# A graph attention layer on one core: the left scores spread over the partitions by two small transposes and a line in DRAM

## The reference

```python
type_sum = adj @ h0                                  # the b side aggregates h0, then multiplies by W_gcnb
attn_a = sigmoid(concat([type_sum, h0]) @ Wa.T + ba)
attn_b = sigmoid(concat([type_sum, h0]) @ Wb.T + bb)
h = h0 @ W_sa
scores = (h @ a_left)[:, None] + (h @ a_right)[None, :]
e = where(adj != 0, exp(-leaky_relu(scores, 0.01)), 0)
x_a = (e / (sum(e, axis=1) + 1e-5)) @ h
x_b = adj @ (h0 @ W_gcnb) + b_gcnb
out = x + sigmoid(attn_a * x_a + attn_b * x_b)
```

## Time and profile before

| | us |
|---|---|
| median of 3 runs | 181.63 |
| lowest and highest | 180.57, 183.06 |
| the profiled execution | 181.05 |
| its span, first to last instruction | 179.3 |
| PE busy in the span | 173.6 |
| DVE, ACT, POOL busy | 146.9, 116.6, 18.3 |

### The profile page before, as it was taken

One profiled execution on the slowest core, in us unless ns is written; L12 is line 12 of the kernel. 1 busy time (PEld: TensorE's weight loads), 2 busy tenths in 40 slices (PEclk: granted clock), 3 DMA queues, 4 the chain that ended last, 5 costly groups with the idle time before them and its releaser, 6 DMA issues.

```text
span 179.3 us, 3430 instructions
## 1 busy us (share of the span) xinstructions
PE 173.6 (97%) x1337; PEld 127.4 (71%) x1337; DVE 146.9 (82%) x309; ACT 116.6 (65%) x171; POOL 18.3 (10%) x42
## 2 busy tenths in 40 slices
PE   7889999999999999999999999999999999999992
PEld 2456676664544448888854478888888888888892
DVE  3698997638899999799999910999999999987542
ACT  3397989753999988658495630584884785773410
POOL 3645346030000200000000000000000000000000
PEclk9999999999999999999999999999999999999999
DMA  6999999999950598000001100000010010011101
GB/s 140 273 249 195 200 179 175 199 239 236 260 212 4 79 214 176 0 4 2 0 4 59 59 0 4 0 0 4 0 59 4 2 59 0 4 60 59 62 29 29
DMA packets 5199, 15.81 MB, mean 88 GB/s; under 512 B 576, under 2 KB 1344, under 8 KB 4416
## 3 DMA queue, kind: packets, MB, share of 16 engines
q0 software_dynamic: 1584, 8.39, 24.4%
q1 hardware_dynamic: 3600, 7.22, 12.0%
HBM read 21.90 MB, written 2.10 MB: 134 GB/s over the span
## 4 chain that ended last, share of the span: by engine, by line
PE 92%; DMA 3%; DVE 2%; SPq 1%; ACT 0%; issue 0%; DVEq 0%
PE ps L762 31%; PE ps L787 16%; PE ps L786 16%; PE ps L785 16%; PE ps L778 6%; PE ps L736 5%; DMA c_sb<-in_consts 3%; PE ps L725 2%; PE ps L747 1%; SPq L225 1%; PE ps L844 1%; DVE stats L475 0%; DVE nat_lo L510 0%; SPq L230 0%; DVE e_lo L505 0%
## 5 line engine op out<-in xcount | busy, mean ns | idle before, releaser
L785 PE MATMUL ps<-mv_lo,e_hi 128*128 128x257 f16 (+2 forms) x272 | 71.0, 267 | 0.0
L787 PE MATMUL ps<-mv_hi,e_lo 128*128 128x257 f16 (+2 forms) x272 | 70.9, 266 | 0.0
L786 PE MATMUL ps<-mv_hi,e_hi 128*128 128x257 f16 (+2 forms) x272 | 70.8, 266 | 0.0
L351 ACT ACTIVATE z<-z,log_e 128x1024 f32<-128x1024 f32 x32 | 36.7, 1146 | 28.6 <-DVE z L547 28.6
L762 PE MATMUL ps<-adj,nat_hi 128*128 128x512 f16 x128 | 48.5, 379 | 0.6 <-DVE nat_lo L510 0.6
L762 PE MATMUL ps<-adj,nat_lo 128*128 128x512 f16 x128 | 48.5, 379 | 0.0
L547 DVE SCALAR_TENSOR_TENSOR z<-sl_row,exs,far 128x512 f32<-128x512 f32 x64 | 45.1, 745 | 0.0
L555 DVE TENSOR_TENSOR e_lo<-z,e_hi 128x1024 f16<-128x1024 f32 x32 | 39.0, 1219 | 1.3 <-ACT e_hi L361 1.3
L361 ACT ACTIVATE e_hi<-z 128x1024 f16<-128x1024 f32 x32 | 33.3, 1041 | 0.0
L786 PEld LDWEIGHTS ps<-mv_hi,e_hi 128*128 128x128 f16 x272 | 26.6, 98 | 3.2
L785 PEld LDWEIGHTS ps<-mv_lo,e_hi 128*128 128x128 f16 x272 | 26.4, 97 | 3.3
(11 more groups left out here) (69 smaller groups left out, 184.1 us busy)
## 6 DMA issues: line engine op xcount, KB each, us to landing
adj<-in_adj_t POOLq DMA_DIRECT2D x6, 1024.0 KB, 10.4
x_sb<-in_x SPq DMA_DIRECT2D x6, 512.0 KB, 13.8
out<-res SPq DMA_DIRECT2D x7, 256.0 KB, 2.0
adj<-in_adj_t POOLq DMA_DIRECT2D x3, 512.0 KB, 8.8
x_sb<-in_x SPq DMA_DIRECT2D x3, 256.0 KB, 5.1
adj<-in_adj_t POOLq DMA_DIRECT2D x2, 256.0 KB, 6.3
wa_sb<-in_w_wide SPq DMA_DIRECT2D x1, 258.0 KB, 4.8
c_sb<-in_consts SPq DMA_DIRECT2D x1, 258.0 KB, 5.0
```

The costliest lines, as they stand in the source:

```text
L351: act.activation(z[:, n % ZRING, :, :], z[:, n % ZRING, :, :], ACT.Exp, bias=log_e[:, 0:1], scale=SLOPE - 1.0).then_inc(exp_done, 1)
L785: pe.matmul(ps[:, bank, cols], e_hi[:, s, i1], mv_lo[:, j, cols], start=(j == 0), stop=False)
L786: pe.matmul(ps[:, bank, cols], e_hi[:, s, i1], mv_hi[:, j, cols], start=False, stop=False)
L787: return pe.matmul(ps[:, bank, cols], e_lo[:, s, i1], mv_hi[:, j, cols], start=False, stop=(j == NT - 1))
```

## The change

The left scores take another way to sl_row. A transpose `sl_lines(h)` turns eight tiles' SL columns at once (in: 128 partitions x 8; out: 8 partitions x 128, in the last quarter of PSUM bank 2 or 0, which no product uses). ScalarE copies the 8 x 128 values to sl_turn, a piece of part_b that is still free. SP stores them as half a line of 2048 values in DRAM, waits for that, and loads the half line back, broadcast to all 128 partitions (512 KB into sl_row).

The first transpose stands ahead of the wide products of tile 10, the second after the first four neighbour tiles of `b_products(1)`. VectorE waits at n = 0 for the first half line and at n = 16 for the second. On ScalarE the first copy stands in `mv_highs(5)`, the second ahead of wg_hi. On SP the second store stands ahead of the `x_back` loads and the second broadcast load behind them.

```diff
+SL_UNIT = 6
+SL_BANKS = (2, 0)
+SL_COLS = slice(BANK - P, BANK)
...
+        sl_turn = [part_b[0:NT // 2, h, 0:P] for h in range(2)]
...
+            def sl_store(h):
+                sp.wait_ge(sl_moved, h + 1)
+                sp.dma_start(sl_line[h * N // 2:(h + 1) * N // 2].rearrange("(t i) -> t i", i=P), sl_turn[h]).then_inc(sl_stored[h], 16)
+
+            def sl_spread(h):
+                sp.wait_ge(sl_stored[h], 16)
+                half = slice(h * N // 2, (h + 1) * N // 2)
+                sp.dma_start(sl_row[:, half], sl_line[half].partition_broadcast(P)).then_inc(sl_ready[h], 16)
+
+            sl_store(0)
+            sl_spread(0)
+            sl_store(1)
             sp.wait_ge(turned, NU)
             sp.wait_ge(nat_ready, NPAIR)
             for g in range(NG):
                 ts = slice(g * GT, (g + 1) * GT)
                 sp.dma_start(x_sb[:, ts, :], x[:, ts, :]).then_inc(x_back[g], 16)
+            sl_spread(1)
...
             def mv_highs(p):
                 act.wait_ge(exs_ready, p + 1)
+                if p == SL_UNIT - 1:
+                    sl_lines(0)
...
-            def sl_rows(c):
-                act.wait_ge(sl_turned, c + 1)
-                act.activation(sl_row[:, c * CW:(c + 1) * CW], ps[:, c % 2, :], ACT.Copy).then_inc(sl_ready, 1)
+            def sl_lines(h):
+                act.wait_ge(sl_turned, h + 1)
+                act.activation(sl_turn[h], ps[0:NT // 2, SL_BANKS[h], SL_COLS], ACT.Copy).then_inc(sl_moved, 1)
...
             act.activation(factor_l[:, :], exs[:, :, SL], ACT.Exp, scale=SLOPE).then_inc(factors_done, 1)
-            sl_rows(0)
-            sl_rows(1)
+            sl_lines(1)
             act.wait_ge(wg_landed, 16)
...
-                if n == 1:
-                    sl_rows(2)
-                    sl_rows(3)
...
                 if j == 0:
-                    dve.wait_ge(sl_ready, c + 1)
+                    dve.wait_ge(sl_ready[c // 2], 16)
...
+                    if t == UNITS[SL_UNIT][0]:
+                        sl_lines(0)
...
-            def sl_rows(c):
-                pe.wait_ge(exs_ready, 2 * c + 2)
...
-                for t in range(GT):
-                    ins = pe.transpose(ps[:, c % 2, t * P:(t + 1) * P],
-                                       exs[:, c * GT + t, SL:SL + 1].broadcast_to([P, P]), ident[:, :])
-                ins.then_inc(sl_turned, 1)
+            def sl_lines(h):
+                pe.wait_ge(exs_ready, 4 * h + 4)
+                pe.transpose(ps[0:NT // 2, SL_BANKS[h], SL_COLS], exs[:, h * NT // 2:(h + 1) * NT // 2, SL],
+                             ident[:, :]).then_inc(sl_turned, 1)
...
                 if p == 0:
-                    pe.wait_ge(sl_ready, NG)
+                    pe.wait_ge(sl_moved, 2)
...
-            sl_rows(0)
-            sl_rows(1)
-            b_products(1, 0, 8)
-            sl_rows(2)
-            sl_rows(3)
-            b_products(1, 8, 16)
+            b_products(1, 0, 4)
+            pe.wait_ge(h0t_ready, NU)
+            sl_lines(1)
+            b_products(1, 4, 16)
             b_products(2, 0, 16)
```

More of the change, by code:

```diff
@@ L65, in piece_of, with build @@
     return next(i for i, (pc, lo, hi) in enumerate(ADJ_PIECES) if pc == c and lo <= j < hi)
-def build(nc, x, adj_t, w_wide, w_post, consts, rows, out):
+def build(nc, x, adj_t, w_wide, w_post, consts, rows, sl_line, out):
     with ExitStack() as ctx:
@@ L175, in build @@
         sl_turned = sem("sl_turned")
-        sl_ready = sem("sl_ready")
+        sl_moved = sem("sl_moved")
+        sl_stored = [sem(f"sl_stored{h}") for h in range(2)]
+        sl_ready = [sem(f"sl_ready{h}") for h in range(2)]
         xh_ready = sem("xh_ready")
@@ L900 @@
     out = nc.dram_tensor("out", (P, NT, D), F32, kind="ExternalOutput").ap()
-    build(nc, *args, out)
+    sl_line = nc.dram_tensor("sl_line", (N,), F32, kind="Internal").ap()
+    build(nc, *args, sl_line, out)
     got = run_bass_kernel_spmd(nc, [arrays], core_ids=[0])
```

## The result

| | before | after |
|---|---|---|
| median of 4 runs, us | 181.1 (180.29 to 183.06) | 184.53 (184.32 to 184.76) |
| ratio, 95% interval | | 1.0205 (1.0153 to 1.0257) |
| span of the profiled execution | 179.3 | 182.5 |

What follows compares the result with a forecast made beforehand. PE, busy in 97% of the span, was taken as the bound. A 3.9 us stall against a 1.5 us gain gave +2.4, on the median of 181.63 a forecast of 184.0 us, range 180.4 to 186.6.

Steps and rivals of the forecast that it cites:

- The gain on PE: On TensorE 16 transposes go (1.74 us) and two come (0.22 us): a gain of 1.52 us, all on the path.
- The load: The 512 KB broadcast load of the half line on SP's queue beside adj pieces: 11.0 us, bounds 4.9 and 12.5.
- its twin: The first x_back load, same shape and size, issued at 33.34 in the same company: 11.0 us.
- The store: SP's 4 KB store of the half line to DRAM: 4.0 us, bounds 1.5 and 7.
- z of n = 0: On VectorE, waiting for store and broadcast load: start at 47.45 us instead of 42.04.
- agg_lo as PE's only tie, one for one: Ahead of b_products(2): z's lateness beyond 43.6 us stalls PE one for one through agg_lo; a stall of 3.9 us.
- the rival: Late, and the clock falls: about 8 products after a 4 us stall cost 1.7 us; net +4.1, 185.7; chance 0.23.
- PEclk falls after the gap: Sign that the forecast is wrong: PE's granted clock drops after its idle time ahead of b_products(2).
- x_back: Reload of x on SP, queued behind the broadcast: the first, wanted by ScalarE at 55.8 us, in time by about 1 us.
- the second half line: The second broadcast into sl_row, wanted at n = 16 near 90 us: covered.
- the e chain's slack: Low part of n = 7 ahead of a_pair(0): 7.1 us of slack, still 4 after the change.
- wg_hi behind the second copy: On ScalarE wg_hi waits behind the second copy: start at 41.66 instead of 40.08 us, z at 43.6 at best, 1.6 later.

Runs made afterwards that it cites:

- other_row: Changed kernel with z reading the constants tile instead of sl_row and waiting only for the constants, all transfers kept: 179.34 us, ratio 0.9933 to the kernel before.
- adj_late: Changed kernel with the two adj pieces of chunk 2 issued only after the first half line has landed: 179.46 us, ratio 0.9929 to the kernel before.
- agg_early: Changed kernel with the high and low parts of chunk 0's aggregate ahead of z of n = 0: 179.43 us, ratio 0.9932 to the kernel before.
- agg_early_5: The changed kernel with chunk 0's aggregate parts ahead of z of n = 0, run again beside a combination: 179.33 us, ratio 0.9916 to the kernel before.
- no_store: Changed kernel whose first broadcast reads a row of x of the same size without waiting for the store: 179.72 us, ratio 0.9947 to the kernel before.
- before_agg_early: The kernel before with chunk 0's aggregate parts ahead of z of n = 0: 181.04 us, ratio 1.0011 to the kernel before.
- double_load: Changed kernel with a second 512 KB broadcast load ahead of the first half line, z waiting for both: 187.84 us, ratio 1.0377 to the kernel before.
- adj6_late: Changed kernel with chunk 2's adj pieces and chunk 1's second one waiting for the first half line: 181.18 us, ratio 0.9995 to the kernel before.
- both: Changed kernel with chunk 0's aggregate parts ahead of z and chunk 2's adj pieces held until the first half line landed: 179.56 us, ratio 0.9921.
- wg_first: Changed kernel with chunk 2's adj pieces held until the first half line landed, and wg_hi ahead of the second copy on ScalarE: 179.51 us, one run.
- warm_gap: Changed kernel with ten products of 512 columns filling PE's idle time ahead of b_products(2): 183.34 us, ratio 1.0155 to the kernel before.

## Why the prediction was right

- **The gain on PE**, -1.52 us from 14 transposes. The runs in which PE waits for nothing at the half line (other_row, adj_late, agg_early) are 1.0 to 1.1 us faster than before by the medians, agg_early_5 is 1.6. The intervals of their ratios, 0.7 to 1.8 us for agg_early and 1.0 to 2.1 for agg_early_5, hold the 1.52. The trace shows it directly, in the start of b_products(2) less its gap. Right.
- **The load**, taken as 11.0 from its twin in the same company: 10.25, in no_store 11.7. Right. The Trainium skill's fit ("DMA: Bandwidth & Descriptors", section "Anatomy of one DMA — SWDGE (gpsimd) path"), 2.0 us plus the bytes at 436 GB/s for a DMA of the other queue, gave an estimate of 5.2 us for store and load. The pair took 5.9 us alone and 15.3 in company, so it was right to set the fit aside.
- **The store**, taken as 4.0: 5.05. The reasoning behind it, a part of the company's cost by the number of rows, was wrong: beside one piece it took the same 5.0 us as beside three, and most of the excess comes before the first packet. That the sum of both came out within 0.3 us is luck, the load's 0.75 on the other side.
- **z of n = 0** at 47.45: 46.84, of an execution whose prologue was 0.76 us early; from the first transpose it is 17.9 us after and was forecast as 17.8.
- **agg_lo as PE's only tie, one for one**: right, by agg_early, before_agg_early and double_load. Stall forecast 3.9, measured 3.97.
- **The clock.** Here the forecast's mechanism lacked a part. The sum left the clock out and had it as part of the rival, 1.7 us for eight matmuls at half rate. "PEclk falls after the gap" was one of the prediction's own signs of being wrong, and that sign came: 1.6 us in the profiled execution, the mean clock down in all four. That is the term that the sum lacks: +2.4 and +1.6 are +4.0, which is the difference between 180.57 and 184.53 and that of the two profiles without the prologue's 0.77. The rival's sum, +4.1, was the better one.
- **The number.** 184.0 came within 0.5 us of 184.53 by luck. It stood on a median of 181.63, of three executions with the 183.06 among them, 1.1 us above the 180.57; the same +2.4 on that would have been 183.0. The half clock should have been in the forecast: a gap forecast at 3.9 us was about to be the longest in the kernel by far, and the rival had priced one of 4.
- **The size of the half clock's price** came from warm-up products 0.43 us apart, in a stretch for which the trace before gives a PEclk of 1.00, so the reading as half clock was an inference. In after the two stand side by side, 0.43 us and 0.50.
- **x_back, the second half line, the e chain's slack**: in the changed kernel no wait names them. Right. The margin of x_back, forecast as about 1 us, is thin: in adj_late, adj6_late, both and wg_first, where adj pieces come later, ScalarE waited for it, by 1.7 to 5.5 us in all, and PE for none of that.
- **wg_hi behind the second copy**, forecast as 1.6 us later than before: 1.5 (40.82 in an execution 0.76 early, for 40.08). wg_first shows the copy as the cause, and in the changed kernel it is hidden behind the broadcast.

## What to carry to other kernels

Where an engine's list is full, count what hangs on the instruction that gets the new wait: here z waited for a DMA, and an unrelated aggregate queued behind it held PE. Putting that aggregate ahead of the wait turned 2% slower into 0.7 to 0.8% faster. Price a transfer by a twin in the same company, never by its size alone, even a tiny one; and add to every forecast gap on PE the matmuls behind it that may run at half clock (here they did behind 4.0 us and not behind 1.5).

## What the runs showed of the hardware that was not expected

- A store of 4 KB from 8 partitions took 1.7 us alone and 4.9 to 5.3 us beside a running 1 MB load of the other queue. In seven of nine runs it landed within 0.2 us of that load, in agg_early and wg_first 1.5 and 1.7 us before it. Its first packet came 3.4 us after its issue in after, 0.8 alone (adj6_late). The broadcast of 512 KB took 3.7 to 4.1 us alone and 10.25 to 11.7 beside 1 MB pieces.
- The granted clock fell to 0.50 behind gaps of 4.0 and 7.3 us and stayed at 1.00 behind PE's waits of 0.6 us (no_store) and 1.5 us (adj6_late), and behind one of 1.7 us that followed filler products (warm_gap); behind both of the long ones the next eight or so matmuls of 512 columns cost 0.43 us each.
- A transpose of 8 columns, whose weight load took 87 ns instead of 137, holds PE as long as one of 128: 0.11 us to the next start.
